# Attention stage of a fused audio tower: one DRAM place per batch for the Q and K halves, and another order of DMA issues on SyncE

## The reference

```python
h = tok(x)                                  # strided conv + mean of pairs + layer norm -> 32 x 188 x 256
h = h + attn(layernorm(h))                  # 16 heads of 16, scores * exp(-0.01|i-j|), softmax, W_o
h = h + ffn(layernorm(h))                   # 16 experts, capacity 2T/16, plus a shared GELU-gated layer

q = x @ W_q; latent = (x @ W_k + x @ W_v) @ W_down_kv
k_rec, v_rec = latent @ W_up_k, latent @ W_up_v          # split into 16 heads
scores = (q k_rec^T / sqrt(256)) * decay
out = (softmax(scores) @ v_rec) @ W_o
```

## Time and profile before

| | |
|---|---|
| runs of the kernel | 2210.71 us (2209.63 to 2211.4) |
| profiled execution, device time | 2226.03 us |
| its span, first to last instruction | 2224.2 us |
| mean granted TensorE clock | 0.90 of full speed |
| busy over the span: PE, DVE, ACT, POOL | 1832.2, 1230.6, 915.5, 929.4 us |
| attention stage, about 157 to 827 us: DMA share in its steady part | 0.52 |

### The profile page before, as it was taken

How to read it: one execution, slowest core, us unless ns; L and a number is a source line. 1 busy time by engine, 2 the same in 40 slices (tenths; PEclk the granted TensorE clock), 3 DMA queues, 4 the chain that set the end, 5 groups by cost and what they waited for, 6 DMA issues and landing times.

```text
span 2224.2 us, 47763 instructions
## 1 busy us (share of the span) xinstructions
PE 1832.2 (82%) x15898; PEld 1346.6 (61%) x15898; DVE 1230.6 (55%) x3686; ACT 915.5 (41%) x1894; POOL 929.4 (42%) x889
## 2 busy tenths in 40 slices
PE   5947889898888854439999295999999899999997
PEld 5944566666556534427777294766666666666665
DVE  4866778888788743325554632445444544544442
ACT  4534556565566532113332112444444444433342
POOL 3841333333333320002222002566666666666655
PEclk9978999999999975559999555999999999999999
DMA  5614455555455521110000003233343333333312
GB/s 161 211 28 91 105 120 121 122 122 121 115 123 124 119 55 33 46 46 22 29 29 30 9 2 134 82 106 86 89 104 89 86 89 100 89 85 88 85 26 28
DMA packets 211856, 186.32 MB, mean 84 GB/s; under 512 B 157136, under 2 KB 192464, under 8 KB 205648
## 3 DMA queue, kind: packets, MB, share of 16 engines
q1 hardware_dynamic: 184912, 141.12, 23.7%
q0 software_dynamic: 26880, 44.36, 9.4%
HBM read 134.51 MB, written 50.44 MB: 83 GB/s over the span
## 4 chain that ended last, share of the span: by engine, by line
issue 31%; POOL 17%; DMA 16%; SPq 15%; PE 11%; DVE 4%; PEld 4%; ACT 2%; POOLq 1%; DVEq 0%; ACTq 0%; PEldq 0%
SPq L416 12%; POOL arena L566 6%; DMA q_halves<-arena 5%; DMA score_table<-arena 4%; DMA out<-hidden,arena 4%; POOL arena L592 4%; PEld psum L1487 4%; POOL out L601 3%; PE psum L1523 3%; SPq L447 2%; PE psum L1540 1%; POOL hidden L505 1%; POOL arena L510 1%; DMA arena<-k_halves 1%; ACT arena L637 1%
## 5 line engine op out<-in xcount | busy, mean ns | idle before, releaser
L566 POOL TENSOR_TENSOR arena<-arena 128x376 f16<-128x376 f32 x320 | 350.7, 1186 | 577.3 <-ACT arena L637 561.0
L1523 PE MATMUL psum<-arena,hidden 128*128 128x376 f16 x3072 | 504.1, 324 | 42.5 <-DVE arena L1192 41.6
L1523 PEld LDWEIGHTS psum<-arena,hidden 128*128 128x128 f16 x3072 | 296.8, 98 | 245.6 <-DVE arena L1192 62.9
L637 ACT ACTIVATE arena<-arena 128x376 f16<-128x376 f32 (+5 forms) x642 | 304.2, 476 | 120.0 <-POOL arena L549 60.4
L982 DVE CUSTOM_DVE_ANT_0 arena<-psum,constants 128x188 f32<-128x188 f32 x768 | 230.2, 349 | 143.6 <-PE psum L1257 142.6
L1192 DVE SCALAR_TENSOR_TENSOR arena<-psum,arena 128x376 f32<-128x376 f32 x256 | 140.3, 548 | 283.1 <-ACT arena L822 188.7
L822 ACT ACTIVATE arena<-psum 128x376 f32<-128x376 f32 x256 | 124.0, 484 | 402.0 <-PE psum L1523 396.3
L637 ACT ACTIVATE arena<-psum 128x188 f32<-128x188 f32 (+8 forms) x467 | 173.8, 400 | 255.8 <-PE psum L1409 46.4
L1540 PE MATMUL psum<-hidden,arena 128*128 128x256 f16 (+1 forms) x2304 | 256.7, 273 | 15.2 <-POOL arena L566 15.2
L1540 PEld LDWEIGHTS psum<-hidden,arena 128*128 128x128 f16 (+1 forms) x2304 | 229.0, 103 | 39.8 <-POOL arena L566 18.3
L527 POOL TENSOR_TENSOR arena<-arena 128x376 f16<-128x376 f32 x128 | 115.4, 902 | 213.0 <-ACT arena L637 210.4
(11 more groups left out here) (152 smaller groups left out, 2951.7 us busy)
## 6 DMA issues: line engine op xcount, KB each, us to landing
arena<-q_halves SPq DMA_DIRECT2D x384, 47.0 KB, 2.2
arena<-k_halves SPq DMA_DIRECT2D x384, 47.0 KB, 2.4
arena<-e_g SPq DMA_DIRECT2D x16, 1024.0 KB, 5.0
arena<-e_u SPq DMA_DIRECT2D x16, 1024.0 KB, 5.2
arena<-e_d SPq DMA_DIRECT2D x16, 1024.0 KB, 5.1
arena<-x_t SPq DMA_DIRECT2D x32, 376.0 KB, 3.4
weighed<-arena POOLq DMA_DIRECT2D x32, 376.0 KB, 4.0
token_table<-arena SPq DMA_DIRECT2D x8, 799.0 KB
```

Of the source, the lines that this page charges most:

```text
L566: nc.gpsimd.tensor_tensor(dst, f, hi, ALU.subtract).then_inc(ready, 1)
L637: return nc.scalar.activation(dst, src, ACT.Copy, scale=scale)
L1523: last = mm(bank[2 * (s % 2) + i][:, 0:CHUNK], w_, a, start=n == 0, stop=n == 5)
```

## The change

Each batch gets its own place in DRAM for Q and for K, so a Q write no longer waits for the reads of an earlier batch. In the hardware loop the addresses of the 24 reads and two writes now depend on the loop's register. The Q write of b+3 moves ahead of the four broadcast reads of the inverted sums, and the K write of b+3 stands at the end of the iteration, directly before the QD reads of the next. Ahead of the QD reads there is a new wait for the plain scores of batch b (the last readers of that tile), and behind nearly every wait a `hold`.

```diff
-    q_dram, k_dram = ([nc.dram_tensor(f"{n}_halves{i}", (2, 2, 128, S), F16) for i in range(2)] for n in ("q", "k"))
+    q_dram, k_dram = (nc.dram_tensor(f"{n}_halves", (B, 2, 2, 128, S), F16) for n in ("q", "k"))
...
-                        sp.dma_start(dst, rows(dram[par], h2, lows[r])).then_inc(landed[par], 16)
+                        sp.dma_start(dst, rows(dram, c, h2, lows[r])).then_inc(landed[par], 16)
+
+            def write(dram, c, halves, low_ready, landed):
+                if valid(c):
+                    sp.wait_ge(low_ready, c + 1)
+                    hold(sp)
+                    sp.dma_start(dram[c, :, :, :, :].rearrange("l c p n -> p (l c) n"), halves.rearrange("p (m n) -> p m n", m=4)).then_inc(landed, 16)
 
             def spread_halves(b, par):
                 c = b + 2
                 if valid(c):
-                    sp.wait_ge(kl_ready, c + 1)
-                    sp.dma_start(k_dram[par][:, :, :, :].rearrange("l c p n -> p (l c) n"), KS2.rearrange("p (m n) -> p m n", m=4)).then_inc(k_out, 16)
                     if isinstance(c, int) and c < 2:
                         sp.wait_ge(blanks_in, 16 * 9)
                     sp.wait_ge(q_out, 16 * c + 16)
-                    read(QD, None, q_dram, (0, 1, 0), par, s_in)
+                    hold(sp)
+                    at_least(sp, s_done, HP * (c - 1))
+                    hold(sp)
+                    read(QD, None, q_dram, c, (0, 1, 0), par, s_in)
                     sp.wait_ge(k_out, 16 * c + 16)
-                    read(None, KX, k_dram, (0, 0, 1), par, s_in)
+                    hold(sp)
+                    read(None, KX, k_dram, c, (0, 0, 1), par, s_in)
                 if valid(b + 1):
                     at_least(sp, st_done, HP * b)
                     hold(sp)
-                    read(None, QX, q_dram, (0, 1, 0), 1 - par, st_in)
+                    read(None, QX, q_dram, b + 1, (0, 1, 0), 1 - par, st_in)
                 c = b - 1
                 if valid(c):
    ...
                 if valid(b + 1):
-                    read(KD, None, k_dram, (0, 0, 1), 1 - par, st_in)
-                c = b - 1
+                    read(KD, None, k_dram, b + 1, (0, 0, 1), 1 - par, st_in)
+                write(q_dram, b + 3, QS, ql_ready, q_out)
                 if valid(c):
                     sp.wait_ge(rs_out, 16 * c + 16)
+                    hold(sp)
                     at_least(sp, on_ready, c)
                     hold(sp)
...
-                c = b + 3
-                if valid(c):
-                    if not isinstance(c, int) or c >= 2:
-                        sp.wait_ge(st_in[1 - par], 96 * c - 96 * (1 - par))
-                        hold(sp)
-                    sp.wait_ge(ql_ready, c + 1)
-                    sp.dma_start(q_dram[1 - par][:, :, :, :].rearrange("l c p n -> p (l c) n"), QS.rearrange("p (m n) -> p m n", m=4)).then_inc(q_out, 16)
+                write(k_dram, b + 3, KS2, kl_ready, k_out)
```

More of the change, by code:

```diff
@@ L403, in _, with rows, read @@
             meet(sp)
-            def rows(dram, h2, low):
-                return dram[low, :, :, :].rearrange("c (a h d) n -> h d (c a) n", h=2, d=HD)[h2]
-            def read(blocks, dense, dram, lows, par, landed):
+            def rows(dram, c, h2, low):
+                return dram[c, low, :, :, :].rearrange("c (a h d) n -> h d (c a) n", h=2, d=HD)[h2]
+            def read(blocks, dense, dram, c, lows, par, landed):
                 for h2 in range(2):
```

## The result

| | before | after |
|---|---|---|
| timed runs, same chip | 2212.24 us (2209.63 to 2219.95, 13 runs) | 2221.65 us (2214.89 to 2229.14, 13 runs) |
| profiled execution | 2226.03 us | 2223.93 us |
| mean granted TensorE clock | 0.90 | 0.898 |

The ratio after / before is 1.0041 [1.0028, 1.0055]: 0.4% slower, where 0.8% faster was forecast, and outside the range. One of the 13 runs after, 2463.24 us at a granted clock of 0.711, ran in a slower state and counts neither for the range above nor for the ratio.

A forecast was written before the change was run, and what follows sets the result against it. SyncE's read issue and the Q write's landing bound the kernel; with them shortened, the loop of sums (18.85, 18.7 taken, against 19.31 us) binds: 28 x 0.6 = 17 us off, 2194 timed (2209 profiled). Range 2175 to 2216, forecast's own 2182 to 2206.

The forecast's parts named there:

- The bound of before: SyncE in the attention stage: issuing its reads and writes, then waiting for the Q write to land, 19.68 us a cycle.
- SyncE's own cycle: SyncE's DMA issues per batch plus the Q write's landing: to fall from 19.68 us to between 16.4 and 18.25.
- The loop of sums: Transposes, inverted sums' write, broadcast reads, GpSimd's multiplication, ScalarE, next transposes: to become the bound at 18.85 us, 18.7 taken.
- four stretches: Transposes to sums' write 7.14, to first broadcast read 4.54, to multiplication 4.9, to next transposes 2.27 us.
- Register addresses: Addresses of SyncE's DMAs from the loop's register: 0.1 us a batch taken, bounds 0 and 3.9.
- From first broadcast read to multiplication: Stretch from SyncE's first broadcast read to GpSimd's multiplication: 4.9 us taken, bounds 4.3 and 6.0.
- so I take 18.7, a little under the sum: Period per batch, taken below the summed 18.85 us; against 19.31 a gain of 0.6 a batch, 17 us in all.
- rival 2: No change: first broadcast read to multiplication takes 5.2 to 5.4 us, or moves show on KD reads; 2207 to 2212; 14%.
- the follower: From GpSimd's multiplication through ScalarE's step to TensorE's next transposes: 0.98 + 1.29 us, 2.27 predicted.
- Rival 3: Slower: the Q write's packets delay the broadcast reads behind it by about 1.2 us; loop 19.75, 2223 us; 11%.
- Rival 4: Slower: each of 26 SyncE DMAs pays 0.15 us for register addresses; cycle 21.15, 2262 us; 5%.
- Rival 1: TensorE becomes the bound: with broadcast reads quicker, 4.0 to 4.3 us, both bind at about 18.1; 2177 us; 10%.

The follow-up runs named there:

- e: Before, with GpSimd multiplying the heads by themselves, without waiting for the broadcast inverted sums: 2218.53 us, 1.0001 to before.
- d: After, with GpSimd multiplying the heads by themselves, without waiting for the broadcast inverted sums: 2187.72 us, 0.9871 to before.
- b: After's order and holds, but two static DRAM buffers as before and QX on its own semaphore: 2226.82 us, 1.0046 to before.
- n: After, with KD reads ahead of the sums' write, ScalarE's high_out at j = 1 and two static DRAM buffers: 2194.69 us, 0.9904 to before.
- a: After, with the Q write put back behind the four broadcast reads, own DRAM places kept: 2237.64 us, 1.0086 to before.
- c: Before, with the six QX reads moved between the K write and the QD reads: 2215.18 us, 0.9996 to before.
- o: Before, with a hold behind five of its waits and the new wait for the plain scores with its hold: 2224.02 us, 1.0035 to before.
- h: After, with ScalarE's high_out, its step behind the multiplication, moved from j = 0 to j = 1: 2200.35 us, 0.9939 to before.
- p: After, with a second, useless Q write of the same data directly behind the first: 2272.42 us, 1.0253 to before.

## Why the prediction was wrong, point by point

**What held.** The bound of before (e against d). SyncE's own cycle: the Q write landed in 2.9 to 3.5 us, and SyncE came early to the inverted sums. The loop of sums as the next bound, and three of its four stretches: 7.13 against 7.14 in nearly all batches, 4.57 against 4.54, 2.24 against 2.27. The Q write goes 0.3 behind the KD reads and doesn't wait for its low half. Register addresses cost nothing measurable where SyncE waits anyway (b, n).

**The step that failed** is "From first broadcast read to multiplication I have 4.63 to 5.73 measured and take 4.9", and behind it "so I take 18.7, a little under the sum". The stretch measures 5.23. The choice rested on the idea that the Q write behind the reads had made the long cases, so that moving it away would help. It did not. With the write behind, the mean is 5.01 to 5.17 in the three profiles of before, 5.00 in a, 4.87 in c and 4.81 in o; with it directly in front it is 5.23 in after, 5.22 in h and 5.49 in b. So the write in front hurts at least as much as the one behind did, which is what rival 2 needed and the prediction held against it. The prediction took 4.9 from three batches; with before's own means over 24 batches, 5.17 for this stretch and 2.52 for the follower, its sum is 7.14 + 4.54 + 5.17 + 2.52 = 19.37, no change. That this is so near to the 19.36 measured is in part luck, since the follower was 0.28 shorter and the clock took 0.18. A window of after with the Q write's packets, then one with the broadcast reads alone (columns as above):

```profile
521.50:522.25 0.75, 0.63 (x12) 0.23 (x9) 0.69 (x4) 0.69 (x2) 0.00 (x0) 1.00 0.90 245
522.25:524.50 2.25, 1.81 (x25) 1.10 (x21) 2.25 (x15) 0.93 (x3) 0.90 (x1) 1.00 0.21 54
```

The write is through by 522.25, 1.0 us after the first broadcast read; the rest of the stretch is the reads' own, at 0.21 of the engines. The Trainium skill, "DMA: Bandwidth & Descriptors", section "Why a DMA increments its semaphore by 16 and not by 1", says that a DMA uses the largest number of engines, up to 16, that divides the slowest dimension of both sides; with four heads as that dimension it is four. The 0.21 here and the 0.24 of rows 9 agree.

**The size of the miss.** The loop is 19.36, not 18.7: 0.33 from the stretch above, 0.18 from batches at half the clock, 0.15 from the rounding down of the sum. That is 28 x 0.66 = 18.5 us, the whole forecast gain of 17. The profiled execution takes 2223.9 instead of 2209. The second part: the prediction carried the 15.3 us by which before's profile lay over its timed runs to the changed kernel. After's profile lies 2.3 over its median, so 13 us more. 15 + 13 makes the 28 us between 2194 and 2221.65.

**No change in the profile, slower in the timed runs.** The first profile of before and that of after have the same period, and rival 2 (5.2 to 5.4 in this stretch, loop 19.15 to 19.35) describes the trace of after. Yet the timed runs are 0.4% or 9.4 us apart. By the profiles part of this lies in the attention stage, outside the table: its 24 batches leave out the first and the last ones. The sums' writes of all 32 batches, in before and then in after (ns min/median/max, first and last start in us):

```profile
L437 SPq DMA_DIRECT2D inverse_sums<-arena x32: 474/496/521, 221.9 to 820.0; - x32
```
```profile
L445 SPq DMA_DIRECT2D inverse_sums<-arena x32: 474/507/512, 218.6 to 820.7; - x32
```

From the first to the last it is 602.1 us in after and 598.1 in before, in whose other two profiles 594.1 and 595.2: after needs 4 to 8 us more. What lies outside took 1620.0 us in after and 1623.9 to 1626.1 in the three of before, which hides it in the profiled totals. Whether these 4 to 6 us outside are scatter of one profile or due to the change (after's first write comes 2.2 to 3.3 us earlier) is open, and so is the rest of the 9.4.

**The other rivals.** Rival 3 had the sign and, by chance, the time (2223), but not the mechanism: the stretch is 5.23, not over 5.4, and a whole extra write makes 0.3, not 1.2. Rival 4 is refuted for after by b; its mechanism costs about 0.5% where SyncE binds (a less o). Rival 1 is refuted: TensorE stands 1.1 us a batch at the transposes and does 18.23 a batch in d.

## What to carry to other kernels

When a change takes a wait from the binding loop, its gain is the distance to the next loop, and that distance must be summed from means over the stage and not from a few batches: here it was 0.6 by three batches and nothing by all 24. A step moved off one loop stands on another; price it there in full (here 0.85 for the Q write, seen as 4.57 against 3.72), and change the two loops together: the same order with the follower one step later (h) is faster than before by 0.6%. A profiled execution is one execution: it lay between 3.1 us under and 13.8 over the median of its kernel here. A forecast of 1% needs more than one profile, and must not carry the excess over to the changed kernel.

## What the runs showed of the hardware

- *TensorE's clock in a nearly always busy stage.* A stand of 1.49 us ahead of the transposes was followed by a granted clock of 0.56 from 548.70 to 552.10, a stand of 1.01 by 1.00 from 529.00 to 532.40; elsewhere in after a stand of 1.57 had no such drop, so the stand alone doesn't decide (in p even one of 2.75 had none). A drop costs the inversion 1.3 to 1.6 us in after and 1.4 to 2.7 in p, where half of the batches have one. A wait added to a loop through TensorE can so cost twice its length: p's 0.87 of added stretches came with 0.88 of clock.
- *Broadcast reads* from four heads each keep only about a quarter of the DMA engines at work (0.21 to 0.24) and need 2.9 us from the end of the last issue to the multiplication in the batch shown of after. From the first issue to the multiplication the means are 4.8 to 5.2 with the Q write behind them, 5.2 to 5.5 with it directly ahead, and 5.5 with two ahead.
- *Issue pace.* Back-to-back reads on SyncE go out every 0.47 us; a MOVE of 29 ns, and a hold in part, disappear in that pace, while behind a landed DMA they show: the next read starts 0.03 us after the landing in before, 0.24 in o with two holds and a wait between, 0.34 in a with the register's address as well.
